# One factor of a product moved from DVE to ACT, the product to POOL, and another order for the last tiles

## What is computed

```python
x = x + xattn(layernorm(x), ctx)       # 16 heads of 64, 154 keys, softmax, then Wo and bo
xq = fp4(layernorm(x))                 # blocks of 16: scale = max|x|/6, round to the fp4 grid, times scale
gate, up = xq @ fp4(w_gate).T, xq @ fp4(w_up).T      # 704 columns each
h = silu(gate) * up
x = x + fp4(h) @ fp4(w_down).T
```

## Time and profile before

| | |
|---|---|
| median of three executions | 912.17 us (910.47 to 912.39) |
| the profiled execution, its own time | 915.48 us |
| span of its trace, first to last instruction | 913.4 us |
| PE busy | 842.0 us (92%) |
| DVE busy | 714.8 us (78%) |
| POOL busy | 540.8 us (59%) |
| ACT busy | 523.8 us (57%) |
| mean granted clock of TensorE | 0.981 |

### The profile page before, as it was taken

The page is one execution under the profiler, slowest core; times in us unless marked ns, Lnnn a source line. Parts: engine busy times, 40 slices in busy tenths (PEclk is TensorE's granted clock), DMA queues, the critical chain, the costliest instruction groups (busy, mean ns, idle before and its releaser), DMA issues.

```text
span 913.4 us, 21461 instructions
## 1 busy us (share of the span) xinstructions
PE 842.0 (92%) x6254; PEld 806.2 (88%) x6254; DVE 714.8 (78%) x2157; ACT 523.8 (57%) x1878; POOL 540.8 (59%) x810
## 2 busy tenths in 40 slices
PE   4786899999999999989999999989999999999984
PEld 4766889999988999989988999989988999999874
DVE  5659788878777888867878888876877888887786
ACT  4544565666665566646656565656665665566530
POOL 6438676764545666646553666665644566665643
PEclk9989999999999999999999999999999999999997
DMA  8101000001010000001010000000100000000000
GB/s 240 43 17 44 7 19 13 24 8 47 8 36 25 11 23 9 23 16 42 13 36 19 14 24 13 17 14 14 48 7 19 13 18 19 12 17 13 7 6 17
DMA packets 20151, 23.22 MB, mean 25 GB/s; under 512 B 2658, under 2 KB 18250, under 8 KB 20042
## 3 DMA queue, kind: packets, MB, share of 16 engines
q1 hardware_dynamic: 20042, 21.94, 8.0%
HBM read 17.74 MB, written 4.19 MB: 24 GB/s over the span
## 4 chain that ended last, share of the span: by engine, by line
PE 65%; DVE 21%; issue 6%; ACT 4%; POOL 2%; DVEq 0%; ACTq 0%; POOLq 0%
PE ps_q L1160 10%; PE ps_s L1202 8%; PE ps_g L1245 8%; PE ps_t L1212 6%; PE ps_o L1225 5%; PE ps_o L1227 5%; PE ps_o L1226 5%; PE ps_g L1123 3%; DVE pT_lo L737 3%; DVE negmax L884 3%; DVE scales L764 3%; PE ps_m L1259 3%; PE ps_m L1261 2%; PE ps_m L1260 2%; ACT probs L678 2%
## 5 line engine op out<-in xcount | busy, mean ns | idle before, releaser
L511 POOL TENSOR_TENSOR probs<-probs,rsum 128x308 f32<-128x308 f32 x256 | 180.4, 705 | 265.2 <-DVE rsum L848 257.3
L678 ACT ACTIVATE probs<-ps_s,negmax 128x154 f32<-128x154 f32 x512 | 194.8, 386 | 218.3 <-DVE negmax L884 217.0
L884 DVE TENSOR_REDUCE negmax<-ps_s 128x2 f32<-128x308 f32 x256 | 121.1, 473 | 91.2 <-PE ps_s L1202 90.7
L1225 PE MATMUL ps_o<-B_sb,pT_lo 128*128 128x256 f32 x640 | 180.9, 283 | 0.9 <-DVE x_both L939 0.6
L1227 PE MATMUL ps_o<-B_sb,pT_hi 128*128 128x256 f32 x640 | 180.7, 282 | 0.0
L1226 PE MATMUL ps_o<-B_sb,pT_hi 128*128 128x256 f32 x640 | 180.4, 282 | 0.0
L737 DVE TENSOR_TENSOR pT_lo<-ps_t,pT_hi 128x256 fp32r<-128x256 f32 (+1 forms) x256 | 122.8, 480 | 34.0 <-ACT pT_hi L572 33.6
L1212 PE MATMUL ps_t<-ident,probs 128*128 128x128 f32 x640 | 113.8, 276 | 26.2 <-DVE pT_lo L737 23.8
L1245 PE MATMUL ps_g<-WGU,xqT_hi 128*128 128x352 f32 x504 | 131.8, 343 | 2.2 <-DVE B_sb L737 1.9
L1225 PEld LDWEIGHTS ps_o<-B_sb,pT_lo 128*128 128x128 f32 x640 | 121.0, 189 | 1.4 <-issue 0.8
L1227 PEld LDWEIGHTS ps_o<-B_sb,pT_hi 128*128 128x128 f32 x640 | 121.5, 190 | 0.0
(11 more groups left out here) (224 smaller groups left out, 2221.2 us busy)
## 6 DMA issues: line engine op xcount, KB each, us to landing
xa<-in_x_dram SPq DMA_DIRECT2D x33, 128.0 KB, 2.1
xr<-in_x_dram SPq DMA_DIRECT2D x32, 128.0 KB, 2.0
out_dram<-y_xn SPq DMA_DIRECT2D x30, 128.0 KB, 1.7
W_sb<-in_L_xattn_Wk_dram SPq DMA_DIRECT2D x4, 512.0 KB, 3.5
W_sb<-in_L_xattn_Wv_dram SPq DMA_DIRECT2D x3, 512.0 KB, 3.7
probs<-in_L_xattn_Wq_dram SPq DMA_DIRECT2D x2, 512.0 KB, 8.5
Wo_sb<-in_L_xattn_Wo_dram SPq DMA_DIRECT2D x1, 1024.0 KB, 9.6
VT<-in_L_ffn_w_down_dram SPq DMA_DIRECT2D x2, 352.0 KB, 3.4
```

What stands on the lines that cost most here:

```text
L511: pool.tensor_tensor(unit, unit, rsum[:, 2 * u:2 * u + 2].unsqueeze(2) .to_broadcast([P, 2, M]), ALU.mult).then_inc(norm_p, 1)
L678: ins = act.activation(probs[:, h, 0:M], ps_s[k % 2][:, s * M:(s + 1) * M], ACT.Exp, bias=negmax[:, h:h + 1], accum_out=sums[:, h:h + 1])
L884: dve.tensor_reduce(negmax[:, 2 * k:2 * k + 2], ps_s[k % 2][:, 0:UM].rearrange("p (h m) -> p h m", h=2), AX_X, ALU.max, negate=True).then_ ...
L1225: pe.matmul(ps_o[:, 0:C], lo[:, j, :], w[:, 0:C], start=first, stop=False)
```

## The change

In the steps (not in `finish`) ACT now takes the up half of a quarter out of the bank, times 0.5, straight into `eh`; then it writes tanh into the small buffer `gu` instead of `eh`. DVE makes the factor in place in `gu`. A new function `times_up` on POOL multiplies the quarter of `eh` by `gu`, in slots 4 to 7, one slot after DVE's silu, and before what POOL has in those slots besides `normalise`. DVE's `hidden` is gone; `largest` waits for POOL instead. PE may refill a bank after silu, and no longer waits for the product. In `finish`, DVE takes the low parts of tile S and of part 0 of T ahead of part 2; PE runs the down product of S and the first third of that of T before it turns parts 1 and 2; and PE gets 8 and 16 matmuls whose results nobody reads (`busy`).

```diff
@@ -511,6 +511,11 @@
+            def times_up(n, q):
+                quarter = slice(q * QF, (q + 1) * QF)
+                pool.wait_ge(silu_v, Q * n + q + 1)
+                pool.tensor_tensor(eh[:, quarter], eh[:, quarter], gu[:, q % 2, :], ALU.mult).then_inc(h_v, 1)
             def quantise_hidden(n, stages):
...
@@ -532,6 +537,8 @@
                         quantise_hidden(d, (k - 1,))
+                    if gate and 4 <= k < Q + 4:
+                        times_up(f, k - 4)
                     if isinstance(t, int) and t == 0 and k == 1:
...
@@ -670,7 +677,12 @@
                         act.wait_ge(gu_mm, Q * f + q + 1)
-                        act.activation(eh[:, quarter], ps_g[q % 2][:, 0:QF], ACT.Tanh, scale=0.5).then_inc(th_a, 1)
+                        act.activation(eh[:, quarter], ps_g[q % 2][:, QF:2 * QF], ACT.Copy, scale=0.5)
+                        if some(Q * f + q - 1):
+                            act.wait_ge(h_v, Q * f + q - 1)
+                        elif q == 0:
+                            act.wait_ge(raw_p, 3 * CHUNKS)
+                        act.activation(gu[:, q % 2, :], ps_g[q % 2][:, 0:QF], ACT.Tanh, scale=0.5).then_inc(th_a, 1)
                     if own:
...
@@ -849,16 +861,9 @@
-                quarter = slice(q * QF, (q + 1) * QF)
                 dve.wait_ge(th_a, Q * n + q + 1)
-                dve.scalar_tensor_tensor(gu[:, q % 2, :], eh[:, quarter], 1.0, ps_g[q % 2][:, 0:QF],
+                dve.scalar_tensor_tensor(gu[:, q % 2, :], gu[:, q % 2, :], 1.0, ps_g[q % 2][:, 0:QF],
                                          ALU.add, ALU.mult).then_inc(silu_v, 1)
-            def hidden(n, q):
-                quarter = slice(q * QF, (q + 1) * QF)
-                dve.wait_ge(silu_v, Q * n + q + 1)
-                dve.scalar_tensor_tensor(eh[:, quarter], ps_g[q % 2][:, QF:2 * QF], 0.5, gu[:, q % 2, :],
-                                         ALU.mult, ALU.mult).then_inc(h_v, 1)
...
@@ -906,8 +911,6 @@
                         layer_norm1(t + 3, 1 - par, pair + 2 + par)
-                    if gate and 3 <= k < Q + 3:
-                        hidden(f, k - 3)
                     if down and k == 0:
...
@@ -1057,15 +1060,16 @@
                 hidden_part(1)
-                gate_by_up(T, 3, ehT, ps_gT[3])
-                largest_of(T, 3, ehT, hriT, am_v)
                 dve.wait_ge(d_mm, R + 1)
...
                 dve.tensor_tensor(y[R % 2], y[R % 2], ps_m[:, 0:C], ALU.add).then_inc(y_v, 1)
-                hidden_part(2)
                 for r in range(2):
                     hidden_lo(S, r)
-                for i in range(3):
+                gate_by_up(T, 3, ehT, ps_gT[3])
+                largest_of(T, 3, ehT, hriT, am_v)
+                hidden_part_lo(0)
+                hidden_part(2)
+                for i in range(1, 3):
                     hidden_part_lo(i)
...
@@ -1232,6 +1236,8 @@
                 if some(Q * f + q - 1):
+                    pe.wait_ge(silu_v, Q * f + q - 1)
+                if isinstance(f, int) and f == S:
                     pe.wait_ge(h_v, Q * f + q - 1)
...
@@ -1260,6 +1266,11 @@
                 return ins
+            def busy(ps, n):
+                for _ in range(n):
+                    pe.matmul(ps[:, 0:C], Wq_sb[0][:, 0, 0:P], Wq_sb[0][:, 0, 0:C], start=True, stop=True)
...
@@ -1301,9 +1312,9 @@
                     if kind == "v" and k < 2:
-                        pe.wait_ge(h_v, Q * f)
+                        pe.wait_ge(silu_v, Q * f)
                     if kind == "k" and k == 7 or kind == "roll" and k >= 6:
-                        pe.wait_ge(h_v, Q * f + (Q if k == 7 else Q - 1))
+                        pe.wait_ge(silu_v, Q * f + (Q if k == 7 else Q - 1))
                     if kind in ("v", "k", "start", "roll"):
...
@@ -1312,6 +1323,14 @@
                         chunk_transposes(turn_at(t, k, 0))
+            def part_transposes(i):
+                if i < 2:
+                    pe.wait_ge(hr_p, 3 * i + 3)
+                else:
+                    pe.wait_ge(hd_v, 3)
+                a = H_PARTS[i][0]
+                transposes(hnT[:, a:a + 2 * P], 2, hT_mm, ps_hT[i])
...
@@ -1330,6 +1349,7 @@
                     transposes(hn[:, 3 * r * P:3 * (r + 1) * P], 3, hqT_mm, ps_hq[r])
+                busy(ps_m, 8)
...
@@ -1345,21 +1365,19 @@
                     transposes(hn[:, 3 * r * P:3 * (r + 1) * P], 3, hqT_mm, ps_hq[r])
-                for i, (a, b) in enumerate(H_PARTS):
-                    if i == 0:
-                        pe.wait_ge(xqT_lo, T + 1)
-                    else:
-                        pe.wait_ge(h_v, Q * T + 2 * i - 1)
-                    if i < 2:
-                        pe.wait_ge(hr_p, 3 * i + 3)
-                    else:
-                        pe.wait_ge(hd_v, 3)
-                    transposes(hnT[:, a:a + 2 * P], 2, hT_mm, ps_hT[i])
+                pe.wait_ge(xqT_lo, T + 1)
+                part_transposes(0)
+                pe.wait_ge(h_v, Q * T + 2)
+                busy(ps_s[1], 16)
                 m_free(None, (y_v, S + 1))
...
                 down_terms(ps_m, *hqT, range(FT)).then_inc(d_mm, 1)
-                pe.wait_ge(h_v, Q * T + 2)
-                for i in range(3):
+                pe.wait_ge(hT_lo, 1)
+                down_terms(ps_s[1], *hqTT, range(2))
+                for i in range(1, 3):
+                    pe.wait_ge(h_v, Q * T + 2 * i - 1)
+                    part_transposes(i)
+                for i in range(1, 3):
                     pe.wait_ge(hT_lo, i + 1)
```

## The result

The changed kernel takes 914.19 us, the median of 20 runs (911.23 to 918.12), beside 912.05 us for the kernel before in 20 runs (909.71 to 915.03): ratio 1.0026, 95% interval 1.0015 to 1.0038. It is 2.4 us slower, 1.4 to 3.5. Forecast were 913.8 us and a loss as the likeliest sign. The total came out right by luck: two of its terms were each wrong by 2.3 us, in opposite directions.

The account below looks back on a forecast made before the run. PE was taken as the bound (92% busy, 65% of the last chain), DVE relief paying only where the chain leaves PE. Steps +3.8 and `finish` -2.2 gave +1.6 us: 913.8 us, range 911.5 to 916.

Parts of the forecast that it names:

- The collision: Slot 0: late `xr + bo` stalls DVE's `scaled`; PE loses 0.21 into odd, 0.18 into even tiles: +1.5, +1.4, +0.6 us.
- this end therefore moves by 0.51 minus the 0.14 gained before it: POOL, slot 7 into slot 0: the end of `xr + bo` comes about 0.37 us later.
- Slot 6: DVE's chain to `power` without `hidden`: gain 0.14 us per even tile, no more; odd tiles (slots 4 and 5) nothing.
- PE runs without a gap: Steady tiles: PE has no idle time except around the change of slot 5 to 6.
- The multiplication: POOL's new 128x176 multiply, slots 4 to 7: 0.55 us each, 0.51 start to start, 120 in all, 66 us.
- POOL dominates: Slower rival: multiply takes 0.70, `scaled` ends 0.4 later, +6 over the steps, 917.2 us; decides from about 0.62; chance 0.18.
- The collision misses: Faster rival: `xr + bo` ends before `scaled` in slot 0, even tiles keep their gain, 908.9 us; chance 0.25.
- Nothing arrives: Rival: DVE's relief hidden, collision absorbed by slack, unread matmuls only fill low-clock time, 912.2 us; chance 0.12.
- ACT's copy: Covered by idle time except slot 5 of tiles 7, 15, 23, where `largest` starts 0.22 later: +0.7 us.
- The `v` tiles' -0.15: Tiles 6, 14, 22: 0.21 later by the copy, 0.37 earlier without `hidden`: -0.15 each, -0.45 us.
- The last tiles: `finish`: new order and unread matmuls start the last add earlier; -2.2 us taken, bounds nothing to -3.1.
- higher clock back before 905: `finish`: sign of a right forecast, PE's 2.4 GHz clock returning before 905 us; the lower level lasted until 907.93.

Follow-up runs that it names:

- the kernel with the two short additions: Kernel before plus two unread 32-column POOL additions in slot 7 ahead of the roundings of xn; run once, profiled, 919.25 us, no ratio.
- the kernels with the addition moved: Whole change with POOL's addition to xr in slot 5 instead of 0, thrown-away matmuls and first tiles varied; ratios to before 0.9973, 0.9984, 0.9985, 0.9976.
- the last two: Whole change, xr addition in slot 5 from tile 3 on: without thrown-away matmuls 0.9985 to before; with only the 8 put back 0.9976.

## Why the prediction came out as it did

**The collision: right in its mechanism and place.** Foreseen were `scaled` at 1.15 us in 15 tiles or more and PE late before the query product of slot 1. It is 1.28 to 1.32 in 17 tiles (4 to 6, 10 to 13, 18 to 21, 26 to 31) and 1.44 once in `finish`. In tile 6 slot 0 grew by nothing all the same. The step that failed is "this end therefore moves by 0.51 minus the 0.14 gained before it". What POOL gains in slot 6, every engine gains, so against `scaled` nothing may be taken off: measured from slot 0's maximum, `xr + bo` ends 0.53 later (1.30 after 0.77). PE then loses 0.43 a tile, into odd and even tiles alike, where 0.35 (0.21 and the 0.14) and 0.18 were forecast. That made +4.5 us with the 0.6 of tiles 3 and 31, and it is +6.8.

**Slot 6: under-read.** Of an even tile 0.14 was forecast and 0.15 measured. For an odd tile the forecast was "nothing", since `hqT_lo` follows ACT in slot 5. That is true of slot 5, whose length did not change. But in slot 6 DVE's chain through `power` to the low part in front of the transposes binds odd tiles too, and they gain the same 0.15. The rows of odd tile 19, the kernel before and then the changed one, show it:

```profile
564.44 0.40 DVE L737 TENSOR_TENSOR pT_lo<-ps_t,pT_hi 128x256 fp32r<-128x256 f32 x1
564.69 0.28 PE L1227 MATMUL ps_o<-B_sb,pT_hi 128*128 128x256 f32 x1
564.99 0.52 PE L1212 MATMUL ps_t<-ident,probs 128*128 128x128 f32 x3
```
```profile
561.12 0.40 DVE L749 TENSOR_TENSOR pT_lo<-ps_t,pT_hi 128x256 fp32r<-128x256 f32 x1
561.55 0.28 PE L1231 MATMUL ps_o<-B_sb,pT_hi 128*128 128x256 f32 x1
561.67 0.52 PE L1216 MATMUL ps_t<-ident,probs 128*128 128x128 f32 x3
```

In both, the transposes start 0.15 us after the low part ends. Before, that was 0.30 after the start of the matmul in front of them, where neighbours start 0.12 apart: PE was 0.18 late. The row names no idle time all the same, since PE's recorded ends are modelled and such an end hides a short wait. "PE runs without a gap" was read from ends that are not measured.

So the collision was forecast 2.3 us too small (+4.5 for +6.8) and the gain of slot 6, the `v` tiles included, 2.3 us too small as well (-1.4 for -3.7). That the two cancelled, +3.8 forecast for the steps and +4.1 measured, is luck.

**The multiplication.** 550 ns forecast from the additions of the earlier trace rows, 563 measured. The Trainium skill, GPSIMD Engine Reference, section 3.1, gives 1.96 times DVE's time for a two-operand addition, measured there at 2048 columns; at 176 columns the trace does not bear this out, since 563 ns are 1.65 times the 341 of DVE's `hidden`, which read one operand from PSUM. The rival *POOL dominates* needed 0.62 and falls. *The collision misses* falls too, and so does *Nothing arrives*: the steps lose 4.1 us, and the ratio is clear of 1.

**ACT's copy.** In the `k` tiles' slot 5 +0.22 was forecast and +0.20 measured. Slot 6 of the same tiles gives 0.15 back, which the forecast left out. The `v` tiles' -0.15 is -0.16.

**The last tiles.** Forecast -2.2, measured -0.7. The part that runs from the turning of part 0 was forecast at -2.2 and is -1.3. Two things were missing. One is the 0.64 us by which the turning of part 0 comes late: the collision returns outside the steps, and the 0.35 without a known cause. The other is the role of the thrown-away matmuls: the forecast left the return of the clock to the work of the 16, and the run with them alone shows no earlier return. In the changed kernel the 16 stand in front of S's matmuls, and the stretch from the turning on takes 10.7 and 10.8 us with the unread matmuls and 10.1 without them. The "higher clock back before 905" did come, by the order.

The sum by stretches is +4.1 - 0.7 = +3.4 us, at the upper end of what the runs say (1.4 to 3.5).

**How the two engines meet.** `scaled` starts 0.16, 0.24 and 0.28 us after a POOL instruction has begun (the changed kernel, the kernel with the two short additions) and ends 0.74 to 0.75 after that one's end each time. The Trainium skill, SBUF — State Buffer, section "two separate sides", describes ports shared by DVE and GpSimd that the one that starts first holds for its whole instruction. The trace agrees with that in order and direction; only the 0.14 us by which `scaled` ends sooner than 0.88 after POOL's end is not explained.

**What stays open.** By stretches, the kernels with the addition moved have steps 1.7 to 2.3 us shorter than before (slot 7 of tiles 13 and 21 left out; 1.5 to 2.0 with it). Their ratios do not lie below that of the new order alone, and for the last two the sum of stretches (-3.6 to -4.1 us for each) is outside the measured intervals (-0.3 to -2.5 and -1.1 to -3.3). The rest must be in what the sum leaves out, among it tile 0, which took 46.5 and 46.1 us in their profiles, or in the difference of the profiled execution from the others. The mean granted clock of their timed executions, 0.985 in both, is close to that of the kernel before beside them (0.987 and 0.985), so it doesn't show the rest. Whether the moved addition has a part in that, or it is chance, one profile of each cannot tell. So moving the multiplication to POOL is shown to be harmless once the collision is gone, not to pay.

## What to carry to other kernels

Before giving work to POOL, look at what POOL's next free-standing instructions run beside on DVE, and measure their ends from an event that all engines share, not in absolute time. An instruction with slack of many slots, such as the addition to xr, should not stand where it only just fits (here within 0.04 us). Before filling idle time with thrown-away matmuls for the clock's sake, run the same places with only the matmuls: here they did nothing, and the order beside them did it all.

## What was not expected of the hardware

PE's granted clock fell after the idle time at the loop's end in some executions of the same steps and not in others, with idle times of 1.7 to 2.4 us on either side, at 1 to 1.8 us each. Together with tile 0 (42.5 to 47 us) this is more than the change itself, and it set the difference of the two profiled executions.

POOL's very short instructions are dear: two operands of 32 columns take 252 ns, beside 563 for 176. With the 737 and 1704 ns of the earlier trace rows for 256 and 704 columns, all four lie within 3 ns of 183 ns plus 2.16 ns a column: an estimate of a fixed part, worked out from these four means.
